# Folding the bias of a mixture of experts into its weights, so that both halves of the relu come straight from PSUM

## The reference, cut to what matters

```
logits = einsum('bsd,de->bse', context, Wg) + bg
scores_topk, idx_topk = top_k(logits, 2)
combine = sum(one_hot(idx_topk, 8) * softmax(scores_topk)[..., None], axis=-2)
h = relu(einsum('bsd,edf->bsef', x, W1) + b1)          # E=8, D=128, F=512
y = einsum('bsef,efd->bsed', h, W2) + b2
out = einsum('bsed,bse->bsd', y, combine)
...
x = x + tanh(g_xattn[0]) * moe0(layernorm(x), ctx_1024, ...)
x = x + tanh(g_ffn[0])   * moe1(layernorm(x), ...)
x = x + tanh(g_xattn[1]) * attention(layernorm(x), ctx_1024, ...)
x = x + tanh(g_ffn[1])   * fp4_mlp(layernorm(x), ...)
```

## Time and profile before

| what | value |
|---|---|
| median of 3 runs | 1567.44 us (1566.91 to 1567.9) |
| profiled execution, its span | 1567.5 us |
| PE busy | 1337.5 us, 85% |
| DVE busy | 1011.9 us, 65% |
| ACT busy | 872.6 us, 56% |
| POOL busy | 716.2 us, 46% |
| chain that ended last | PE 45%, DVE 20%, issue 15%, POOL 10%, ACT 8% |

### The profile page before, as it was taken

One profiled execution on the slowest core, in us unless ns is written; L12 is line 12 of the kernel. 1 busy time (PEld: TensorE's weight loads), 2 busy tenths in 40 slices (PEclk: granted clock), 3 DMA queues, 4 the chain that ended last, 5 costly groups with the idle time before them and its releaser, 6 DMA issues.

```text
span 1567.5 us, 25069 instructions
## 1 busy us (share of the span) xinstructions
PE 1337.5 (85%) x6350; PEld 979.1 (62%) x6350; DVE 1011.9 (65%) x2377; ACT 872.6 (56%) x2421; POOL 716.2 (46%) x971
## 2 busy tenths in 40 slices
PE   7778988889978898879888899888998898896884
PEld 5556766667656766557666676666666576574552
DVE  6866675856668476766758566585666857574442
ACT  5535764556744575447655466455664477553652
POOL 3533554435534355444634355344553446442342
PEclk9979997999989899999989899799997999996765
DMA  3310000000000000000000000000000000000000
GB/s 99 108 41 4 5 9 15 4 6 7 5 14 4 7 8 6 16 6 8 4 20 2 9 4 10 14 4 8 8 6 14 5 9 5 6 3 7 4 4 4
DMA packets 34084, 20.48 MB, mean 13 GB/s; under 512 B 3624, under 2 KB 31888, under 8 KB 33936
## 3 DMA queue, kind: packets, MB, share of 16 engines
q1 hardware_dynamic: 33936, 18.81, 4.2%
HBM read 16.70 MB, written 2.10 MB: 12 GB/s over the span
## 4 chain that ended last, share of the span: by engine, by line
PE 45%; DVE 20%; issue 15%; POOL 10%; ACT 8%; DVEq 1%; POOLq 0%; SPq 0%; DMA 0%; ACTq 0%
PE M L1034 5%; PE U L1051 5%; PE U L877 4%; DVE h_lo L743 4%; PE U L881 4%; PE U L878 4%; PE Y L877 3%; ACT big L648 3%; PE Y L881 3%; PE M L1021 3%; DVE h L739 3%; PE Y L878 2%; PE M L1041 2%; PE M L1065 2%; POOL big L549 2%
## 5 line engine op out<-in xcount | busy, mean ns | idle before, releaser
L743 DVE TENSOR_TENSOR h_lo<-h,h_hi 128x512 fp32r<-128x512 f32 x384 | 316.9, 828 | 72.6 <-POOL h_hi L508 60.0
L508 POOL TENSOR_SCALAR h_hi<-h 128x512 fp32r<-128x512 f32 x256 | 180.5, 707 | 257.7 <-ACT h L609 230.0
L648 ACT ACTIVATE big<-big,nmax 128x128 f32<-128x128 f32 x512 | 199.8, 395 | 88.8 <-DVE nmax L841 88.3
L609 ACT ACTIVATE h<-U,biasT 128x512 f32<-128x512 f32 x256 | 175.9, 687 | 102.5 <-PE U L881 88.9
L549 POOL TENSOR_TENSOR big<-big,rinv 128x512 f32<-128x512 f32 x128 | 150.3, 1174 | 151.7 <-DVE rinv L844 151.7
L1051 PE MATMUL U<-big,Vr 128*128 128x512 f32 x256 | 150.9, 674 | 24.0 <-ACT big L653 24.0
L1034 PEld LDWEIGHTS M<-kT,qT 8*128 8x128 f32 x944 | 116.1, 189 | 84.3 <-issue 69.6
L1034 PE MATMUL M<-kT,qT 8*128 8x128 f32 x944 | 138.7, 286 | 2.2 <-ACT sg L666 2.1
L877 PE MATMUL U<-xn_hi,w_hi 128*128 128x512 f32 x256 | 119.3, 466 | 21.9 <-DVE h L739 12.9
L844 DVE RECIPROCAL rinv<-rsum 128x4 f32<-128x4 f32 x128 | 22.7, 177 | 174.4 <-ACT big L648 174.4
L619 ACT ACTIVATE h_hi<-h 128x512 fp32r<-128x512 f32 x128 | 80.9, 632 | 84.6 <-DVE h L739 81.7
(11 more groups left out here) (210 smaller groups left out, 3023.9 us busy)
## 6 DMA issues: line engine op xcount, KB each, us to landing
big<-in_L_xattn_W SPq DMA_DIRECT2D x16, 256.0 KB, 3.0
big<-in_L_ffn_w SPq DMA_DIRECT2D x12, 256.0 KB, 2.8
xin<-in_x SPq DMA_DIRECT2D x8, 256.0 KB, 2.7
nat<-in_ctx SPq DMA_DIRECT2D x8, 256.0 KB, 3.2
ctx<-in_ctx SPq DMA_DIRECT2D x32, 64.0 KB, 1.8
mask_sb<-in_mask_BxSxS_if SPq DMA_DIRECT2D x32, 64.0 KB, 1.9
out_dram<-xatt SPq DMA_DIRECT2D x32, 64.0 KB, 1.6
big<-in_L_ffn_w_down SPq DMA_DIRECT2D x1, 176.0 KB
```

The source lines that it names most:

```text
L508: nc.gpsimd.tensor_scalar(h_hi[i % 4][:, :], h32[i % 3][:, :], 1.0, 0.0, ALU.mult, ALU.add).then_inc(hi_done, 1)
L609: nc.scalar.activation(h32[i % 3][:, :], U[i % 2][:, :], ACT.Relu, bias=biasT[:, i:i + 1]).then_inc(relu_done, 1)
L648: done = nc.scalar.activation(p, p, ACT.Exp, bias=nmax[:, u % 2, r:r + 1], accum_out=rsum[:, u % 2, r:r + 1])
L743: nc.vector.tensor_tensor(h_lo[i % 4][:, :], h32[i % 3][:, :], h_hi[i % 4][:, :].bitcast(fp32), ALU.subtract).then_inc(lo_done, 1)
```

## The change

The layernorm's output sums to zero over its 128 values, so (x + 1) times a weight column with mean b/128 gives x W + b exactly. The change replaces W1 by W1 - colmean(W1) + b1/128, and feeds x + 1. No bias is left to add in the relu, and so the relu of U can be taken twice: once by ACT, written as fp32r (h_hi), and once by DVE, inside the subtraction that makes h_lo. GpSimd has no part in it any more, and bank U is free only when DVE has read it. The weights are centred in group 0: PE makes M = -mean(W1) + b1/128 by two fp32 matmuls for each expert, and DVE adds it to the staged piece before ACT splits it.

```
-                        nc.gpsimd.tensor_scalar(h_hi[i % 4][:, :], h32[i % 3][:, :], 1.0, 0.0, ALU.mult, ALU.add).then_inc(hi_done, 1)
...
             def split_hi(k):
                 act.wait_ge(staged[k % 4], 16 * (k // 4 + 1))
+                if k < 2 * E0 and k % 2 == 0:
+                    act.wait_ge(centred, k // 2 + 1)
                 nc.scalar.activation(pieces[k][1], big[:, k % 4, :], ACT.Copy).then_inc(wsplit_hi, 1)
...
                     elif what == "up" and i < N0:
                         act.wait_ge(up_done, g * N0 + (i + 1))
-                        if past(g) or i >= 3:
-                            act.wait_ge(lo_done, g * NC + (i - 2))
-                        nc.scalar.activation(h32[i % 3][:, :], U[i % 2][:, :], ACT.Relu, bias=biasT[:, i:i + 1]).then_inc(relu_done, 1)
+                        if past(g) or i >= 4:
+                            act.wait_ge(down_done, g * NC + (i - 3))
+                        nc.scalar.activation(h_hi[i % 4][:, :], U[i % 2][:, :], ACT.Relu).then_inc(hi_done, 1)
...
-                        nc.scalar.activation(xn_hi[i][:, :], Z[:, :], ACT.Copy).then_inc(xnhi_done, 1)
+                        nc.scalar.activation(xn_hi[i][:, :], Z[:, :], ACT.Identity, bias=1.0 - i).then_inc(xnhi_done, 1)
...
             def split_lo(k):
+                if k < 2 * E0 and k % 2 == 0:
+                    dve.wait_ge(staged[k % 4], 16 * (k // 4 + 1))
+                    dve.wait_ge(mean_full, k // 2 + 1)
+                    nc.vector.tensor_tensor(big[:, k % 4, :], big[:, k % 4, :], M[k // 2 % 2][:, :], ALU.add).then_inc(centred, 1)
                 dve.wait_ge(wsplit_hi, k + 1)
...
                         dve.wait_ge(hi_done, g * NC + (i + 1))
-                        nc.vector.tensor_tensor(h_lo[i % 4][:, :], h32[i % 3][:, :], h_hi[i % 4][:, :].bitcast(fp32), ALU.subtract).then_inc(lo_done, 1)
+                        if i < N0:
+                            nc.vector.scalar_tensor_tensor(h_lo[i % 4][:, :], U[i % 2][:, :], 0.0, h_hi[i % 4][:, :].bitcast(fp32),
+                                                           ALU.max, ALU.subtract).then_inc(lo_done, 1)
...
+            def expert_mean(e):
+                k = 2 * e
...
+                pe.wait_ge(staged[k % 4], 16 * (k // 4 + 1))
+                if e >= 2:
+                    pe.wait_ge(centred, e - 1)
+                nc.tensor.matmul(M[e % 2][:, :], spread, big[:, k % 4, :], start=True, stop=False)
+                nc.tensor.matmul(M[e % 2][:, :], b1_by_d[:, e:e + 1].broadcast_to([E0, P]), b1_rows, start=False, stop=True).then_inc(mean_full, 1)
...
+                    elif what == "split":
+                        if i < 2 * E0 and i % 2 == 0:
+                            expert_mean(i // 2)
...
                         if i >= 2:
-                            pe.wait_ge(relu_done, g * N0 + (i - 1))
+                            pe.wait_ge(lo_done, g * NC + (i - 1))
```

More of the change, by code:

```diff
@@ L240, in flamingo_kernel @@
         acc, part = sb("acc", [P, NT]), sb("part", [P, NT])
-        bias_rows = acc[0:N0 + E0, 0:P]
+        bias_rows = acc[0:E0, 0:P]
+        spread = xatt[:, 0, :]
+        b1_rows = xmid[0:E0, :, :].rearrange("p j d -> p (j d)")
         bn0, mv0 = sb("bn0", [P, TG, 6]), sb("mv0", [P, TG, 2])
@@ L476, in _ @@
                                     pattern=[[-1, P]], channel_multiplier=1).then_inc(ident_made, 1)
+            pool.wait_ge(ident_made, 1)
+            nc.gpsimd.tensor_scalar(ident_d[:, :], ident[:, 0:E0], 1.0 / P, 0.0, ALU.mult, ALU.add).then_inc(ident_made, 1)
             def quantise(part, t, q):
@@ L557, in split_hi @@
                 act.wait_ge(staged[k % 4], 16 * (k // 4 + 1))
+                if k < 2 * E0 and k % 2 == 0:
+                    act.wait_ge(centred, k // 2 + 1)
                 nc.scalar.activation(pieces[k][1], big[:, k % 4, :], ACT.Copy).then_inc(wsplit_hi, 1)
             act.wait_ge(z_full, 1)
-            nc.scalar.activation(biasT[:, :], Z[:, 0:N0 + E0], ACT.Copy).then_inc(z_emptied, 1)
+            nc.scalar.activation(biasT[:, :], Z[:, 0:E0], ACT.Copy).then_inc(z_emptied, 1)
             def layer1_weights(w):
@@ L742, in walk @@
                         dve.wait_ge(hi_done, g * NC + (i + 1))
-                        nc.vector.tensor_tensor(h_lo[i % 4][:, :], h32[i % 3][:, :], h_hi[i % 4][:, :].bitcast(fp32), ALU.subtract).then_inc(lo_done, 1)
+                        if i < N0:
+                            nc.vector.scalar_tensor_tensor(h_lo[i % 4][:, :], U[i % 2][:, :], 0.0, h_hi[i % 4][:, :].bitcast(fp32),
+                                                           ALU.max, ALU.subtract).then_inc(lo_done, 1)
+                        else:
+                            nc.vector.tensor_tensor(h_lo[i % 4][:, :], h32[i % 3][:, :], h_hi[i % 4][:, :].bitcast(fp32), ALU.subtract).then_inc(lo_done, 1)
                     elif what == "combine":
@@ L754, in walk @@
                         if i < E0:
-                            ins = nc.vector.scalar_tensor_tensor(dst[:, :], Y[i % 2][:, :], biasT[:, N0 + i:N0 + i + 1], cbc[i % 2][:, :], ALU.add, ALU.mult)
+                            ins = nc.vector.scalar_tensor_tensor(dst[:, :], Y[i % 2][:, :], biasT[:, i:i + 1], cbc[i % 2][:, :], ALU.add, ALU.mult)
                         else:
@@ L790, in walk @@
                         dve.wait_ge(xnhi_done, 2 * g + 3 if i == 0 else 2 * g + 2)
-                        nc.vector.tensor_tensor(xn_lo[i][:, :], Z[:, :], xn_hi[i][:, :].bitcast(fp32), ALU.subtract).then_inc(z_emptied, 1)
+                        nc.vector.scalar_tensor_tensor(xn_lo[i][:, :], Z[:, :], 1.0 - i, xn_hi[i][:, :].bitcast(fp32), ALU.add, ALU.subtract).then_inc(z_emptied, 1)
                     elif what == "logits":
```

26 lines of the change are left out of this document (14 added, 12 removed).

## The result

The changed kernel takes 1592.4 us (median of 4, 1589.85 to 1595.28), the kernel before on the same chip 1567.18 us (4 runs, 1566.1 to 1567.9). The ratio is 1.0148, 95% interval 1.0112 to 1.0183: slower by 1.5%. I had forecast 1575, slower by 0.5%, with a range up to 1588. The direction was right, and so was the new wait in group 0; the size was not, and PE's clock in the later groups was in no term of the sum. The profiled execution's span is 1592.2 us (before 1567.5), close to the median, so its parts can stand for it. (In a later timing 19 runs of the kernel before spread from 1559.65 to 1579.53 us, and so the 3.1 us that the prediction took as what can be told from no change was too small.)

What follows compares the result with a forecast made beforehand. The prediction took PE to bound the first mixture of groups 1 to 7 (busy 99.4 of 107 us). It summed 1567.4 + 21.4 (group 0) - 14.7 (groups 1 to 7) + 0.3 = 1574.4, said 1575 us, range 1560 to 1588.

Steps and rivals of the forecast that it cites:

- xn_hi's identity: Passage to the second mixture, once a group: 598 to 687 ns, at most 0.7 us in all, taken as 0.3.
- The wait of product 4e+2 for h_lo 4e: Group 0: h_lo 4e stands behind the splits in DVE's order, so PE stands 2.28 us for each expert.
- The steady groups' waits: Groups 1 to 7, first mixture: new waits on U against a shorter chain, net -2.1 us a group.
- Rival 1: Groups 1 to 7 win more and outweigh group 0: at 4.5 us a group, 1558 us; chance 0.17.
- Rival 2: Group 0's stall is not there: group 0 costs +7.9 us, total 1561 us; chance 0.08.
- Rival 4: Groups 1 to 7: waits on U are not given back, 0 to +2 us a group, 1589 to 1603; chance 0.10.
- Group 0, +21.4 in the sum: Group 0's first mixture gets longer: 3.2 + 2.1 + 4.0 + 16.7 - 4.6 = +21.4 us.
- the mean's two products at 1.72: Group 0, each expert: two fp32 matmuls on PE at 0.86 us each, within an expert's 10.04 us.
- The first slots: Group 0 before column 6: 3.2 + 2.1 + 4.0, so column 6 is late by 9.3 us.
- rival 3: Group 0: PE's clock falls in seven stalls, 7 x 1.3 = 9 us, total 1584; chance 0.15.
- The tail: Group 0 behind column 26, to the last h_lo: 15.8 us in place of 20.4, or -4.6.
- Groups 1 to 7, -14.7 in the sum: First mixtures of the seven steady groups: 7 x 2.1 us won, -14.7 us of the whole kernel.

Runs made afterwards that it cites:

- Experiment 4: Changed kernel with idle PE products in group 0's stalls, no wait removed: 1588.11 us, ratio 1.0115 to the kernel before.
- experiment 5: Kernel before with idle PE products in the passages and at the end of the loop's body: 1549.27 us, ratio 0.9864 to the kernel before.
- experiment 6: Changed kernel with idle PE products in the passages and at the end of the loop's body: 1561.37 us, ratio 0.9951 to the kernel before.
- experiment 3: Changed kernel with a third PSUM bank for U in group 0: 1580.51 us, ratio 1.0052 to the kernel before.
- experiment 7: Changed kernel with group 0's mean, centring and splits spread over the slots: 1575.37 us, ratio 1.0049 to the kernel before.
- experiment 8: Changed kernel with group 0's centring steps spread and a third bank for U there: 1572.13 us, ratio 1.0018 to the kernel before.
- experiment 11: Changed kernel with each mean's two products made twice, the second pair over the first: 1622.07 us, measured once.
- experiment 9: Changed kernel with spread splits, three U banks in group 0 and idle products in the passages: 1541.79 us, ratio 0.9853 to the kernel before.
- experiment 2: Changed kernel with the centring kept but GpSimd's copy and the relu's chain of before: 1588.66 us, ratio 1.0121 to the kernel before.

## Why the prediction was off

**What held.** The changed durations: relu 597 for 598, h_lo 684 for 690, xn_hi's identity 597 with a number for a bias, so it costs nothing (I took 0.3 in all). h_lo is no longer drawn out beside GpSimd; the row of before that speaks for it, 1.53 us beside a GpSimd product, has no successor. The Trainium skill, SBUF — State Buffer, "SBUF: two separate sides", says that a VectorE instruction with two SBUF inputs and a GpSimd one that reads SBUF hold a shared pair of ports in turn; the trace agrees, as h_lo has one SBUF input now and its longest in group 4 is 693 ns. The wait of product 4e+2 for h_lo 4e came at all of columns 6 to 26, 1.9 to 2.2 us for 2.28. The steady groups' waits moved as I had walked them: products wait for U four times in group 4's stage, 2.3 us in all, the waits for the mask's addition are gone, and its first mixture is 2.0 us shorter. Rivals 1 and 2 fell. Rival 4 fell for the first mixture.

**Group 0, +21.4 in the sum, +29.7 measured.** Four terms were mis-sized.
- An expert took 10.31 us between columns 10 and 26 (one of the four 10.60), not 10.04. The step is the mean's two products at 1.72: they take 2.00, since I used `pv`'s 0.86 from the chain for both, and the second is a product with 8 rows of weights that takes 1.06 in the chain above. That is 0.28 for each of five, 1.4 us, and 0.3 at column 6.
- The first slots: column 6 starts 12.4 late in place of 9.3. The kernel before is at the half clock until 22.7 and then at the full one; the changed one until 11.6, from 15.0 to 21.9 and from 25.3 to 32.1. Its second mean (3.1 us from 19.55 to the next product) and the third one's slots fall in this, and I had allowed the half clock for the first mean alone.
- The step from column 6 to column 10 took 11.87 us, 1.5 more than the others, with a half-clock spell from 38.9. This is rival 3, which I had put beside the forecast and not in it. Experiment 4 prices it: 4.0 us between h_lo 2 and h_lo 31, not the 9 that I gave it, and its condition held after two of the seven waits of 1.9 to 2.2 us (the spells from 38.9 and from 97.0), not after all.
- The tail gave back 2.6 us, not 4.6. The count of DVE's steps was right, the price was not: seven h_lo from PSUM took 680 ns each, but the twelve lo parts of the weights took 865 in the mean in place of 680 (DVE's groups, 91.2 to 109.1 us):

```profile
L702 DVE TENSOR_TENSOR w_lo<-big,w_hi 128x512 fp32r<-128x512 f32 x12 | 9.9, 865 | 1.5 <-ACT w_hi L560 1.5
L750 DVE SCALAR_TENSOR_TENSOR h_lo<-U,h_hi 128x512 fp32r<-128x512 f32 x7 | 4.8, 680 | 0.0
```

  Ten of them took 676 to 693 ns, and the two that began while one of GpSimd's additions for the combine ran took 1765 and 1791: the same drawing out that h_lo has got rid of. I had put's median of 680 where its longest, 1776, stood beside it. 12 x 0.185 is 2.2 us.

**Groups 1 to 7, -14.7 in the sum, -3.9 measured.** The mechanism was right for the first mixtures, -16.8 as I had reckoned them. The step that failed is that the sum carried what they win to the end of the program, with no term for PE's clock in the places between them. In the passage and at the end of the loop PE has waits and the clock falls, and how long it stays down sets how long these places take. In the kernel before the passages of groups 1 to 6 take 21.0 to 24.1 us; the changed kernel has 24.1 in five of these six groups and in group 7, each with a spell of 17.1 us at the half clock. Before, three groups of the seven had 17.1, two had 10.2, and the others 6.8 and 3.4. In these two kernels a spell of 3.4 us goes with a passage of 21.0, 6.8 with 21.8, 10.2 with 23.2 and 23.4, and 17.1 with 24.1. Experiments 5 and 6 price it: with idle products the passage is 20.54 in both kernels, the period is 2.03 shorter in the changed one, and the seven groups come to -15.0. Behind group 0's first mixture the fallen clock costs the kernel before 18 us and the changed one 31. By the table's cuts, from h_lo 2 of group 1 on, the idle products bring 18.8 and 29.9 us, and of these 11.1 us between the two kernels 3.6 lie in the passages, 5.9 at the ends of the loop and in the last stretch, 2.4 in the first mixtures and -0.8 in the second ones. So the passages are a third of it, and no one place has it all. The Trainium skill, TensorE: Matmul & The Clock Gate, "A second HAM failure mode: psum-queue depth-cycling", says that many short idles of PE between groups of matmuls can also lower its clock again and again; here the waits of the passage are 0.3 to 1.9 us each and its granted clock is 0.65 over 24.1 us, but in one long spell, not in many falls.

How firm is the -3.9? The changed kernel's code from group 1 on runs in five more kernels (experiments 3, 4, 7, 8 and 11), and from h_lo 2 of group 1 to the end they take 1407.9 to 1416.8 us, for 1413.9 here and 1417.9 before. So one execution tells this number to some 5 us only. With idle products experiments 6 and 9 have 1384.0 and 1382.5, for 1399.1 before: there the gain is plain.

Also, the second mixture is 0.5 us longer in the changed kernel with the clock kept up too (48.07 for 47.60). In group 4 it comes in two steps, 0.24 at h_lo 35 and the rest at h_lo 43 (experiments 5 and 6, h_lo by h_lo). I did not forecast this. The runs do sort it. In the mean of groups 1 to 6 the nine kernels with the centring take 48.06 to 48.18 us, whichever relu they have (experiment 2 has the old one), and the four without it 47.60 to 47.73. In the nine DVE stands still twice in each of these second mixtures, with nothing that the profile shows it waiting for, and in the four never (timeline of the changed kernel, group 4):

```profile
862.67 0.17 DVE L816 FIND_INDEX8 ix<-mx,lg 128x8 uint32<-128x8 f32 x1 [0.20 <-issue]
...
888.58 0.69 DVE L745 TENSOR_TENSOR h<-U,h 128x512 f32<-128x512 f32 x1 [0.36 <-issue]
```

The centring has no instruction in these groups; only the program ahead of them is longer. Why DVE stands still there is open.

**The range.** It ended at 1588, with rival 3 as its upper side. With group 0 at its measured 29.7 the sum would have been 1582.7, still 10 short: that is the clock in groups 1 to 7. The error was to treat the clock as a rival with one place, and to take as given that what the steady groups win reaches the end.

**Still open.** Why the changed kernel falls into the 17-us spell in every group from the second on. From group 2 to 5 its period repeats to 0.6 us and the spells come 184.3 us apart, so whatever sets it may repeat too. That a saving upstream shifts the later work against the clock's fall and rise is my reading; experiment 4 speaks for it, where the same instructions 2.0 us earlier got shorter spells in four of seven groups and a longer one in group 1. Other shifts made no such difference: in experiments 3, 8 and 11, whose group 1 comes 10 and 16 us earlier and 25 later, all seven passages take 24.1 us. No run shifts a passage by a known amount to test this. The kernel before varied by 20 us over 19 runs on one chip; its longest and shortest passage differ by 3.1 us, so the passages of seven groups alone could just make it, but only one execution is profiled.

## What to carry to other kernels

A one-off stage with weights to prepare can lose more than a loop wins: count one turn of its new chain by the engines' own order, and put the work that the next buffer release waits for ahead of work that nobody needs yet (here: spreading the splits and one more bank took back 16.7 of 29.7 us). Where PE's granted clock in a stage is well below 1 (here 0.78 and 0.65 in the passages), try filling its waits with products that nobody reads; that alone gave 1.4% here. Judge a saving upstream of such a stage with the clock kept up as well, since otherwise the gain of the change and what the clock gives or takes are in one number.

## What the runs showed of the hardware

- Idle products in the passages, some 26 for each group, shortened the kernel by 18 us of span (1567.5 to 1549.3) and raised the mean granted clock from 0.921 to 0.954.
- An fp32 product of 512 columns at the full clock takes 0.95 to 1.05 us start to start, with 8 rows of weights no less than with 128.
- How long the start stays at the half clock differs much between kernels that differ little there: its last early spell ended at 18.3, 22.7, 28.0, 32.1 and 42.3 us (experiment 9, before, experiment 8, changed, experiment 11; the changed kernel had two short stretches at the full clock ahead of that and one more spell from 38.9), and h_lo 2 ended at 24.5, 22.8, 28.9, 26.8 and 36.9. So a difference of a few us in the start of one kernel should not be read as the change's own.
- At the turn of the loop PE and DVE stand still for 2.2 to 3.1 us with nothing that the profile shows them waiting for (2.94 and 2.84 before, group 4); with idle products in front of it PE's idle time there is 0.9 to 1.3 us (experiments 5 and 6).
- A DVE instruction with two SBUF inputs (a lo part of the weights) took 1765 and 1791 ns where it began during a GpSimd addition of 1.65 and 1.68 us, and 676 to 693 ns in the other ten cases, none of which began during an addition.
